# Cross-attention and quantized feed-forward on one core: scores in two float32r parts by pairs of heads, and one ring of seven PSUM banks

## The chip, the cores and the metric

The kernel runs on one core of a Trainium2 chip, in one launch. The metric is the time of an execution on the device in microseconds (us); given is the median of three runs.

## What is computed

There are 16 batches of 512 tokens with 256 values, and for each batch a context of 1601 rows with 192 values. All is float32.

```
x = x + xattn(layernorm(x), ctx)          # 16 heads of 16 values
x = x + ffn(layernorm(x))
xattn: Q = tokens @ Wq; K = ctx @ Wk; V = ctx @ Wv
       softmax(Q K^T * 16**-0.5) V, heads joined, @ Wo + bo
ffn:   fp4_linear(silu(fp4_linear(x, w_gate)) * fp4_linear(x, w_up), w_down)   # 704 wide
       fp4_linear rounds both operands to 4-bit values in blocks of 16, each block with its own scale
```

## The kernel before

**Bodies, groups, steps.** After a start (first context, projections and maxima) there is one body for each batch (first, middle, last), and then a tail for the last batch's feed-forward. A body has four groups of four heads (`PHASES`, `PER_GROUP`), and a group has 13 steps (`KEY_TILES`), each for 128 keys (65 in the last): 52 steps. A step computes, for four heads, the scores of 128 keys against all 512 queries (L901), ACT's exponential of each (L1028), and one step later the sums of the values weighted with them (L912), the four heads in four column strips of the array, with a column of ones beside the values for the softmax's denominator.

**Shift.** So that the exponential can't overflow, each query's largest score is taken off. It is found one group ahead: for each head, four tiles of 128 queries and four pieces of 400 or 401 keys, PE computes the scores the other way round (a "piece", L926, 64 a group) into a ring of three banks, and DVE reduces each to its maximum (L1264). `max_parts` (L1165 to L1173) is five DVE operations that take the maximum over the pieces and cut its negative into three bf16 parts; the round `maxima` transposes them on PE (L845), ACT copies them (L998), and one DMA puts them as three more rows under the stacked queries of the next group (L725), to be multiplied with rows of ones under the keys. The first score of a group waits for this DMA.

**Parts.** Keys and queries are cut into three bf16 parts each (`SPLITS`): ACT copies the projection out of PSUM twice (L984, L987), and POOL takes off and rounds in three operations (L1343 to L1347). SP's DMAs stack the parts of a head in 96 rows, parts of the query repeated 3, 2 and 1 times against the matching parts of the key (`STACK`, L641, L715): six issues a head. A buffer holds four heads and one spare for each parity of the group.

**Rounds.** All other matmuls and transposes are rounds (projections of queries, keys and values, transposes of the context, and for the batch before the output projection and the feed-forward's parts). They use two `work` banks in turn and are drained by ACT or DVE. Float32r operands, with high and low parts, are in the key and value projections (L832, L840) and in the gate and up projection (L865).

**Order.** Every engine walks the same list and does its own part of each item, in order; nothing is reordered at run time. The tables `POST_AT`, `OWN_AT`, `PRE_AT`, `TAIL_AT` and others say at which half step an event is put; an event's rounds are put with it. `sequence` (L277) spreads four scores, the pieces, the rounds and the weighted sums over the step by their cost (`SCORE_PLACE`, `PIECE_WEIGHT`). Scores have a ring of two banks of their own, pieces three, rounds two, and the weighted sums one.

Of the kernel before, what the change touches and what calls it, by code (L numbers as in the profile page):

```python
# [24 lines left out]
F32 = mybir.dt.float32  # L25
# [17 lines left out]
STACK = [3, 2, 1]  # L43
SROWS = sum(STACK) * HEAD_DIM
SHIFT = 3
SPLITS = 3
TINY = 1e-12
ONES_PAIR = struct.unpack("<f", struct.pack("<I", 0x3F803F80))[0]
# [16 lines left out]
]  # L65
TAIL_AT = [
# [15 lines left out]
PIECE_FROM, PIECE_TO = 0.0, 22  # L82


PIECE_WEIGHT = [
# [4 lines left out]
]  # L90
SCORE_PLACE = [0.1225, 0.3125, 0.5225, 0.7625]
PIECE_SHIFT = 0.8
# [11 lines left out]
def events(kind, key_tiles, h_pieces):  # L104
# [24 lines left out]
    for g in range(PHASES):  # L129
        loads = [("stack", (g + 1) % PHASES, j) for j in range(1, PER_GROUP)] + [("stack", (g + 2) % PHASES, 0)] * (g % 2)  # L130
        if kind == "last":
            loads = loads[:3] * (g < PHASES - 1) + loads[3:] * (g < PHASES - 2)
# [7 lines left out]
        if g == PHASES - 1:  # L140
            loads[2:2] = [("load_resid", n) for n in ((0, 1, QT, QT + 1) if kind == "last" else (0, 1))]
# [51 lines left out]
def build(nc, x, ctx_768, Wq, Wk, Wv, Wo, bo, w_gate, w_up, w_down, out):  # L193
# [44 lines left out]
    def splits(of, n, k):  # L238

        return count(of, SPLITS * 2 * (CHUNKS + 1), SPLITS * n + k)  # L240

# [10 lines left out]
    def banks_free(n, ring, per_group):  # L252

        if n >= ring:
            return n - ring + 1
# [1151 lines left out]
```

## Time and profile before

| | |
|---|---|
| median of three runs | 3501.74 us (3499.99 to 3502.39) |
| span of the profiled execution, first to last instruction | 3497.6 us |
| that execution's own time | not given apart from its span |
| mean granted TensorE clock | 0.992 |
| busy: PE, PE weight loads, DVE, ACT, POOL | 97%, 45%, 83%, 66%, 29% |
| chain that ended last: PE, DVE, ACT | 77%, 17%, 2% |
| HBM read and written | 46.22 MB, 8.39 MB |

PE is TensorE's matmuls, PEld its weight loads, DVE VectorE, ACT ScalarE, POOL GpSimd and SP the queue that issues DMAs. Matmuls are pipelined: each has a duration longer than the time until the next one starts, so the distance of two starts tells what one occupies. A row with xN merges N instructions that follow or overlap.

### The profile page before, as it was taken

How to read it: one execution, taken by the hardware profiler on the slowest of the kernel's cores; microseconds unless marked ns; L12 is line 12 of the kernel's file. 1: busy time of each engine (PE TensorE's matmuls, PEld its weight loads, DVE VectorE, ACT ScalarE, POOL GpSimd, SP SyncE). 2: the span in 40 equal slices, each digit the busy share in tenths (PEclk: the TensorE clock that was granted, in tenths of full speed). 3: DMA queues.
4: the chain of work that ended last, by engine and by line, in shares of the span. 5: the costliest groups of instructions: out<-in, count | busy, mean ns of one | idle time of the engine just before them, and what ended most of it. 6: DMA issues, size and time to landing. Idle time of an engine off the chain costs nothing.

```text
span 3497.6 us, 55854 instructions
## 1 busy us (share of the span) xinstructions
PE 3402.9 (97%) x19606; PEld 1557.8 (45%) x19606; DVE 2900.8 (83%) x6561; ACT 2299.7 (66%) x4512; POOL 1001.4 (29%) x1114
## 2 busy tenths in 40 slices
PE   6999999999999999999999999999999999999997
PEld 3334444444444444444444444444444444444434
DVE  6878888888888988888888888988888888888865
ACT  2667666666666667666667666666666666666662
POOL 1323322333222323222333322333222333222213
PEclk8999999999999999999999999999999999999999
DMA  4333233232233332233232232332232231332310
GB/s 85 55 51 50 36 55 54 30 63 41 44 51 46 52 45 47 39 58 49 36 63 34 49 54 36 62 45 42 44 58 44 41 62 30 52 54 32 42 24 8
DMA packets 154262, 163.01 MB, mean 47 GB/s; under 512 B 58071, under 2 KB 127080, under 8 KB 153984
## 3 DMA queue, kind: packets, MB, share of 16 engines
q1 hardware_dynamic: 153984, 159.45, 28.9%
q8 instruction: 157, 2.57, 0.3%
q14 instruction: 121, 0.99, 0.1%
HBM read 46.22 MB, written 8.39 MB: 16 GB/s over the span
## 4 chain that ended last, share of the span: by engine, by line
PE 77%; DVE 17%; ACT 2%; POOL 1%; DMA 1%; issue 1%; SPq 1%; ACTq 0%; DVEq 0%
PE out_ps L912 19%; PE score_ps L901 18%; PE piece_ps L926 17%; DVE piece_max L1264 10%; PE work L865 6%; PE work L876 4%; PE work L832 3%; PE work L840 3%; ACT probs L1028 1%; PE work L821 1%; PE work L856 1%; PE work L873 1%; DVE ctx_T L1134 1%; PE work L850 1%; DVE stats L1107 1%
## 5 line engine op out<-in xcount | busy, mean ns | idle before, releaser
L1028 ACT ACTIVATE probs<-score_ps 128x512 f32<-128x512 f32 (+1 forms) x3328 | 1883.9, 600 | 900.0 <-PE score_ps L901 892.0
L1264 DVE TENSOR_REDUCE piece_max<-piece_ps 128x1 f32<-128x400 f32 (+1 forms) x4096 | 2113.3, 566 | 381.2 <-PE piece_ps L926 367.9
L926 PE MATMUL piece_ps<-k_stack,q_stack 96*128 96x400 bf16 (+1 forms) x4096 | 1291.3, 338 | 27.1 <-DVE piece_max L1264 12.6
L901 PE MATMUL score_ps<-q_stack,k_stack 99*128 99x512 bf16 (+1 forms) x3328 | 1251.7, 384 | 19.3 <-DMA q_stack<-neg_rows 5.2
L912 PE MATMUL out_ps<-probs,v_ones 128*17 128x512 f32 x6656 | 876.6, 599 | 0.4
L926 PEld LDWEIGHTS piece_ps<-k_stack,q_stack 96*128 96x128 bf16 x4096 | 385.1, 98 | 768.9 <-DVE piece_max L1264 514.7
L901 PEld LDWEIGHTS score_ps<-q_stack,k_stack 99*128 99x128 bf16 (+1 forms) x3328 | 324.2, 99 | 646.7 <-ACT probs L1028 494.5
L1316 POOL TENSOR_TENSOR h<-h,h_grid 128x704 f32<-128x704 f32 (+1 forms) x68 | 101.4, 1492 | 881.2 <-DVE h_grid L1092 881.2
L865 PE MATMUL work<-wgu_T,xq_T 128*128 128x512 f32 (+1 forms) x1080 | 333.8, 426 | 0.5
L912 PEld LDWEIGHTS out_ps<-probs,v_ones 128*17 128x17 f32 x6656 | 110.3, 95 | 270.3 <-issue 214.6
L865 PEld LDWEIGHTS work<-wgu_T,xq_T 128*128 128x128 f32 x1080 | 198.1, 191 | 44.0 <-issue 3.8
L1343 POOL TENSOR_TENSOR rest<-rest,k_parts 128x512 f32<-128x512 f32 (+1 forms) x127 | 128.5, 1012 | 266.6 <-ACT rest L987 266.6
L832 PE MATMUL work<-ctx_T,wk_sb 128*128 128x512 f32 (+1 forms) x640 | 199.2, 423 | 5.3 <-DVE ctx_T L1134 2.9
L876 PE MATMUL work<-wd_T,h_T 128*128 128x256 f32 x744 | 190.5, 378 | 0.8 <-ACT h_T L1018 0.8
L840 PE MATMUL work<-wv_sb,ctx_T 128*128 128x256 f32 (+1 forms) x1040 | 187.8, 314 | 1.9 <-DVE wv_sb L1124 1.9
L840 PEld LDWEIGHTS work<-wv_sb,ctx_T 128*128 128x128 f32 (+1 forms) x1040 | 150.4, 188 | 21.2 <-issue 2.8
L876 PEld LDWEIGHTS work<-wd_T,h_T 128*128 128x128 f32 x744 | 138.9, 190 | 25.9 <-ACT h_T L1016 1.0
L1355 POOL TENSOR_TENSOR rstd<-mean_var,eps 128x1 f32<-128x1 f32 x64 | 15.1, 235 | 458.7 <-DVE mean_var L1198 458.7
L1316 POOL TENSOR_TENSOR xq<-xq,h_grid 128x256 f32<-128x256 f32 x60 | 40.2, 670 | 360.8 <-DVE h_grid L1092 360.8
L1008 ACT ACTIVATE tanh_g<-work 128x256 f32<-128x256 f32 (+1 forms) x192 | 70.4, 367 | 102.9 <-PE work L865 100.8
L832 PEld LDWEIGHTS work<-ctx_T,wk_sb 128*128 128x128 f32 x640 | 115.0, 194 | 28.9 <-issue 3.2
L1347 POOL TENSOR_TENSOR k_parts<-rest,k_parts 128x512 bf16<-128x512 f32 (+1 forms) x127 | 114.4, 901 | 9.9
(170 smaller groups left out, 2711.4 us busy)
## 6 DMA issues: line engine op xcount, KB each, us to landing
k_stack<-k_parts SPq DMA_DIRECT2D x256, 150.1 KB, 3.6
k_stack<-k_parts SPq DMA_DIRECT2D x256, 100.1 KB, 3.9
ctx_in<-in_ctx SPq DMA_DIRECT2D x47, 384.0 KB, 3.7
k_stack<-k_parts SPq DMA_DIRECT2D x256, 50.0 KB, 3.7
q_stack<-q_parts SPq DMA_DIRECT2D x256, 48.0 KB, 2.8
x_in<-in_x SPq DMA_DIRECT2D x16, 512.0 KB, 5.0
q_stack<-q_parts SPq DMA_DIRECT2D x256, 32.0 KB, 2.1
resid<-in_x SPq DMA_DIRECT2D x62, 128.0 KB, 3.3
```

The lines of the kernel that those rows point to most:

```text
L832: last = pe.matmul(work[:, 0:w], wk_sb[:, by, e * P:(e + 1) * P], ctx_T[:, of, a:a + w], start=(n == 0), stop=(n == len(PRODUCTS) - 1))
L840: last = pe.matmul(work[0:r, u * D:(u + 1) * D], ctx_T[:, of, a:a + r], wv_sb[:, by, :], start=(n == 0), stop=(n == len(PRODUCTS) - 1))
L865: last = pe.matmul(work[:, 0:w], quarter(kind, t).xq_T[:, of, k, :], wgu_T[:, k, by, a:a + w], start=(k == n == 0), stop=(k == 1 and n == ...
L876: last = pe.matmul(work[:, 0:D], quarter(kind, event[1]).h_T[:, c, :], wd_T[:, c, :], start=(c == 0), stop=(c == FT - 1))
L901: pe.matmul(score_ps[0:r, n % SCORE_RING, :], k_stack[:, par, slot(g, j), m * P:m * P + r], q_stack[:, par, slot(g, j), :], start=True, st ...
L912: last = pe.matmul(out_ps[32 * j:32 * j + V1, :], v_ones[0:r, batch % 2, m, PER_GROUP * g + j, :], probs[0:r, step % 2, j, :], start=(m == ...
L926: pe.matmul(piece_ps[:, n % PIECE_RING, 0:hi - lo], q_stack[0:SROWS, par, slot(g, j), t * P:(t + 1) * P], k_stack[0:SROWS, par, slot(g, j) ...
L1028: act.activation(probs[0:r, step % 2, j, :], score_ps[0:r, (PER_GROUP * m + j) % SCORE_RING, :], ACT.Exp, scale=SCORE_SCALE).then_inc(prob ...
L1264: dve.tensor_reduce(piece_max[:, row, c:c + 1], piece_ps[:, n % PIECE_RING, 0:piece_at[c + 1] - piece_at[c]], AX_X, ALU.max).then_inc(piec ...
L1316: pool.tensor_tensor(src, src, grid, ALU.add).then_inc(done, 1)
L1343: pool.tensor_tensor(left, left, parts[:, 0, a:a + w], ALU.subtract).then_inc(split_step, 1)
L1347: pool.tensor_tensor(parts[:, 2, a:a + w], left, parts[:, 1, a:a + w], ALU.subtract).then_inc(split_step, 1)
```

## The change

Keys and queries are cut into two float32r parts. ACT still copies the projection twice, and POOL has one operation. A head has 48 rows (the query's high part twice and low part once, against the key's high, low and high) and two rows for the shift, which has two float32r parts, too. Of each pair of heads the even one lies in rows 0 to 49, the odd one in rows 64 to 113, of five buffers that the pairs use in turn; scores and pieces of a pair stand next to each other in the list. `max_parts` has three operations, and the shift goes out in four DMAs. All of PSUM but the bank of the weighted sums is one ring of seven, taken in the order of the list: each score, piece or round claims the bank that the seventh one before it used, and waits for its drain. Pieces are 402 wide, the last overlapping. A step's order is now fixed, and the tables are new.

```diff
-STACK = [3, 2, 1]
-SROWS = sum(STACK) * HEAD_DIM
-SHIFT = 3
-SPLITS = 3
+SROWS = 3 * HEAD_DIM
+SHIFT = 2
+HALF = P // 2
+PAIRS = PER_GROUP // 2
+PAIR_SLOTS = 5
 POST_AT = [
+    [4, 5, 5, 9, 13, 14, 19, 20, 20, 21, 23, 23, 23, 26, 33, 34, 38],
+    [22, 23, 23, 23, 32, 37, 38, 43, 45, 45, 48, 48, 51, 51, 56, 62, 65],
+    [52, 55, 55, 58, 59, 59, 65, 66, 66, 66, 68, 69, 70, 73, 78, 80, 85],
+    [74, 74, 74, 74, 74, 78, 82, 86, 86, 87, 87, 93, 95, 95, 100, 101, 102],
 ]
-OWN_AT = [8, 13, 14, 16, 18]
-PRE_AT = [26, 28, 31, 33, 37, 37, 41, 42, 46, 47, 48, 49, 59, 62, 66, 69, 71, 73, 80, 85, 94, 94]
-STACK0_AT = [15, 65]
-LN1 = 5
-HEADS_OUT_AT = 1
+OWN_AT = [6, 13, 14, 17, 18]
+PRE_AT = [26, 28, 29, 30, 37, 37, 47, 48, 51, 51, 54, 55, 59, 62, 66, 69, 69, 70, 78, 83, 87, 91]
+STACK0_AT = [17, 71]
+LN1 = 6
+HEADS_OUT_AT = 3
 MAX_AT = [22, 23]
+PIECES_AT = [
+    [3, 3, 4, 3, 2, 3, 3, 3, 3, 3, 2, 0, 0],
+    [3, 3, 3, 2, 3, 3, 4, 3, 3, 3, 2, 0, 0],
+    [3, 3, 3, 2, 3, 3, 3, 3, 3, 3, 3, 0, 0],
+    [3, 3, 4, 4, 4, 1, 3, 3, 2, 3, 2, 0, 0],
 ]
+STEP_ORDER = "S01 P W01 P S23 P V"
+RINGS, RING_FOR = (7,), (0, 0, 0)
+MERGE = (False, False)
...
+                for what in STEP_ORDER.split():
+                    if what == "P":
+                        take = -(-left // (2 * slots)) * 2
+                        left, slots = left - take, slots - 1
+                        for _ in range(take):
+                            put(0, "piece", (g + 1) % PHASES, n)
...
-        k_stack = sb("k_stack", [SROWS + SHIFT, 2, PER_GROUP + 1, KW], BF16)
-        q_stack = sb("q_stack", [SROWS + SHIFT, 2, PER_GROUP + 1, NQ], BF16)
+        k_stack = sb("k_stack", [P, PAIR_SLOTS, KW], F32R)
+        q_stack = sb("q_stack", [P, PAIR_SLOTS, NQ], F32R)
...
-        piece_ps = ps("piece_ps", [P, PIECE_RING, 512], F32)
-        score_ps = ps("score_ps", [P, SCORE_RING, 512], F32)
+        ring = ps("ring", [P, BANKS, 512], F32)
         out_ps = ps("out_ps", [P, 512], F32)
-        work_ps = ps("work", [P, 2, 512], F32)
...
+            def stack_keys(of, g, u):
+                at = pair_slot(of, g, u)
+                for half in range(2):
+                    rows, to = pair_rows(g, u, half)
+                    sp.dma_start(k_stack[to:to + 2 * HEAD_DIM, at, 0:NK].bitcast(F32), k_parts[rows, :, 0:NK]).then_inc(stacked[at], 16)
+                    sp.dma_start(k_stack[to + 2 * HEAD_DIM:to + SROWS, at, 0:NK].bitcast(F32), k_parts[rows, 0, 0:NK]).then_inc(stacked[at], 16)
...
                 elif name == "maxima":
+                    for j in range(PER_GROUP):
+                        to = HALF * (j % 2) + SROWS
+                        row = q_stack[to:to + SHIFT, pair_slot(of, g, j // 2), :].bitcast(F32).rearrange("n (t c) -> n t c", c=P)
+                        sp.dma_start(row, neg_rows[SHIFT * QT * j:SHIFT * QT * (j + 1), :]).then_inc(shift_loaded[g % 2], 16)
...
+            def claim(kind, batch, item):
+                user = bank_user(kind, batch, item)
+                if user:
+                    pe.wait_ge(*released(*user))
...
+                item = ("scores", step, j)
+                claim(kind, batch, item)
+                rows = slice(lo, lo + SROWS + SHIFT)
+                pe.matmul(ring[0:r, bank(kind, batch, item), :], k_stack[rows, at, m * P:m * P + r], q_stack[rows, at, :],
+                          start=True, stop=True).then_inc(scores_ready, 1)
...
+                claim(kind, batch, item)
+                rows, (a, b) = slice(lo, lo + SROWS), piece_at(c)
+                pe.matmul(ring[:, bank(kind, batch, item), 0:PW], q_stack[rows, at, t * P:(t + 1) * P], k_stack[rows, at, a:b],
+                          start=True, stop=True).then_inc(pieces_ready, 1)
...
-                        for par in range(2):
-                            for j in range(PER_GROUP):
-                                act.wait_ge(stacked[par][j], count(batch, 2 * KSTACKED, KSTACKED * (1 if half else 2)))
+                        first = pair(of, 2 * half, 0)
+                        for k in range(first - 2 * PAIRS, first):
+                            act.wait_ge(stacked[k % PAIR_SLOTS], stacked_until(k))
...
-                    pool.tensor_tensor(left, left, parts[:, 0, a:a + w], ALU.subtract).then_inc(split_step, 1)
-                    pool.tensor_tensor(parts[:, 1, a:a + w], left, zero[:].broadcast_to([P, w]), ALU.add).then_inc(split_step, 1)
-                    pool.tensor_tensor(parts[:, 2, a:a + w], left, parts[:, 1, a:a + w], ALU.subtract).then_inc(split_step, 1)
+                    pool.tensor_tensor(low.bitcast(F32R), low, parts[:, 0, a:a + w], ALU.subtract).then_inc(split_step, 1)
```

In `STEP_ORDER`, S01 and S23 are the scores of a pair, P a third of the step's pieces (`PIECES_AT` counts them in pairs), W01 the events of the step with their rounds, and V the weighted sums of the step before. `POST_AT` has a row for each quarter of 128 tokens of the batch before and a place for each of heads_T, out_proj, ln2_stats, ln2_apply, xq_max, xq_scale, xq_T, three gate_up, h_max, h_small, h_scale, h_grid, two h_T and down; `OWN_AT` places one query and four key projections of the batch's second half, and `PRE_AT` two x_T, eight ctx_T, two v_proj, one query and four key projections and five v_proj of the next batch.

## Rows read from the trace of the kernel before

**Rows 1.** The page, parts 1 and 2: busy time of engines; PE's tenths in 40 slices.

```profile
PE 3402.9 (97%) x19606; PEld 1557.8 (45%) x19606; DVE 2900.8 (83%) x6561; ACT 2299.7 (66%) x4512; POOL 1001.4 (29%) x1114
...
PE   6999999999999999999999999999999999999997
```

**Rows 2.** Stages: us, then busy PE, PEld, DVE, ACT, POOL, clock, DMA share, GB/s.

```profile
0.00:75.00 75.00, 47.12 (x195) 27.87 (x196) 48.19 (x112) 16.78 (x34) 13.61 (x25) 0.85 0.39 78
...
1479.00:1690.00 211.00, 209.46 (x1227) 96.37 (x1223) 179.04 (x406) 143.15 (x282) 61.52 (x69) 1.00 0.30 47
```

**Rows 3.** Groups by line, 1479 to 1690: count | busy us, mean ns | idle before.

```profile
L926 PE MATMUL piece_ps<-k_stack,q_stack 96*128 96x400 bf16 (+1 forms) x256 | 80.5, 337 | 0.6 <-DVE piece_max L1264 0.2
L901 PE MATMUL score_ps<-q_stack,k_stack 99*128 99x512 bf16 (+1 forms) x208 | 78.1, 384 | 0.6
```

**Rows 4.** The chain that ended last, in order of time: start us, us, what.

```profile
361.74 1.93 DVE piece_max L1264 x4
...
3102.83 1.93 DVE piece_max L1264 x4
...
1490.71 0.59 SPq L715
1491.34 0.78 SPq L715
1492.16 3.13 DMA q_stack<-neg_rows
```

**Rows 5.** Timeline of PE, 1501 to 1504: start us, us, what.

```profile
1501.59 0.38 PE L901 MATMUL score_ps<-q_stack,k_stack 99*128 99x512 bf16 x1
1501.89 1.05 PE L912 MATMUL out_ps<-probs,v_ones 128*17 128x512 f32 x8
...
1502.34 0.61 PE L912 MATMUL out_ps<-probs,v_ones 128*17 128x512 f32 x4
1502.88 0.68 PE L926 MATMUL piece_ps<-k_stack,q_stack 96*128 96x401 bf16 x3
1503.40 0.38 PE L901 MATMUL score_ps<-q_stack,k_stack 99*128 99x512 bf16 x1
```

**Rows 6.** Timeline of PE, 223 to 225; three of the four transposes again, alone.

```profile
223.84 0.34 PE L926 MATMUL piece_ps<-k_stack,q_stack 96*128 96x401 bf16 x1
224.11 0.46 PE L883 MATMUL work<-ident,h 64*128 64x64 f32 x4
224.50 0.60 PE L901 MATMUL score_ps<-q_stack,k_stack 99*128 99x512 bf16 x2
...
224.11 0.40 PE L883 MATMUL work<-ident,h 64*128 64x64 f32 x3
```

**Rows 7.** Timeline of PE: three float32r matmuls, and the first two of them.

```profile
1513.77 1.01 PE L865 MATMUL work<-wgu_T,xq_T 128*128 128x512 f32 x3
...
1513.77 0.78 PE L865 MATMUL work<-wgu_T,xq_T 128*128 128x512 f32 x2
```

**Rows 8.** Timeline of PEld: three float32r weight loads, and the first two of them.

```profile
1484.38 0.46 PEld L832 LDWEIGHTS work<-ctx_T,wk_sb 128*128 128x128 f32 x3
...
1484.38 0.34 PEld L832 LDWEIGHTS work<-ctx_T,wk_sb 128*128 128x128 f32 x2
```

**Rows 9.** Timeline of DVE in the start, 44 to 71.

```profile
43.91 25.11 DVE L1264 TENSOR_REDUCE piece_max<-piece_ps 128x1 f32<-128x400 f32 x52
...
69.81 0.17 DVE L1171 TENSOR_TENSOR neg_parts<-piece_ps,zero 128x16 bf16<-128x16 f32 x1
70.02 0.17 DVE L1173 TENSOR_TENSOR neg_parts<-piece_ps,neg_parts 128x16 bf16<-128x16 f32 x1
```

**Rows 10.** The chain in the start.

```profile
29.59 1.05 POOL k_parts L1345
```

**Rows 11.** Timeline of ACT in the last group.

```profile
3407.65 2.17 ACT L1028 ACTIVATE probs<-score_ps 128x512 f32<-128x512 f32 x4 [0.43 <-PE score_ps L901]
3410.53 2.17 ACT L1028 ACTIVATE probs<-score_ps 128x512 f32<-128x512 f32 x4 [0.71 <-PE score_ps L901]
```

More of the change, by code:

```diff
@@ L249, in build @@
     R_START, R_FIRST, R_BODY = (len(ROUND[k]) for k in ("start", "first", "middle"))
-    PIECE_RING, SCORE_RING = 3, 2
-    def banks_free(n, ring, per_group):
-        if n >= ring:
-            return n - ring + 1
-        return max(b + 1 for b in range(per_group) if b % ring == n) - per_group
+    BANKS = sum(RINGS)
+    RING_OF = {"scores": RING_FOR[0], "piece": RING_FOR[1], "round": RING_FOR[2]}
     def transposes(event):
@@ L325, in sequence @@
         for g in range(PHASES):
-            steps = []
+            ahead = g < PHASES - 1 or kind != "last"
+            n = 0
             for m in range(KEY_TILES):
-                fill, step = [], g * KEY_TILES + m
-                for part in range(2):
-                    es = EVENTS[kind].get(2 * step + part, [])
-                    for e in es:
-                        fill.append((0, ("event", e)))
-                        if e[0] in ROUNDS:
-                            fill += [(c, ("round", e, i)) for i, c in enumerate(round_parts(e))]
-                    if part == 0 and (step or kind != "first"):
-                        fill.append((4 * NQ, ("weighted", step - 1)))
-                steps.append(fill)
@@ L340, in sequence @@
[L340 to L356 removed]
+                step = g * KEY_TILES + m
@@ new lines, in build @@
+    DRAIN = {k: {e: sum(by_vector(k, o) == by_vector(k, e) for o in ROUND[k] if ROUND[k][o] < n) for e, n in ROUND[k].items()} for k in ROUND}
+    BANK_USERS = {}
+    for k in SEQUENCE:
+        BANK_USERS[k] = [[] for _ in RINGS]
+        for item in SEQUENCE[k]:
+            if item[0] in ("scores", "piece"):
+                BANK_USERS[k][RING_OF[item[0]]].append(item)
+            elif item[0] == "round" and item[2] == 0:
+                BANK_USERS[k][RING_OF["round"]].append(("round", item[1]))
@@ new lines, in build, with before, bank @@
+    FIRST_USE = {k: {item: n for users in BANK_USERS[k] for n, item in enumerate(users)} for k in BANK_USERS}
+    def before(kind, batch, per):
+        at = {"start": [], "first": ["start"], "middle": ["start", "first"] + ["middle"] * (batch - 1),
+              "last": ["start", "first"] + ["middle"] * (B - 2), "tail": ["start", "first"] + ["middle"] * (B - 2) + ["last"]}[kind]
+        return sum(per(k) for k in at)
+    def bank(kind, batch, item):
+        of = RING_OF[item[0]]
+        n = before(kind, batch, lambda k: len(BANK_USERS[k][of])) + FIRST_USE[kind][item]
+        return sum(RINGS[:of]) + n % RINGS[of]
@@ new lines, in body_before, with bank_user @@
+    def body_before(kind, batch):
+        if kind == "tail":
+            return "last", B - 1
+        if kind == "first":
+            return "start", -1
+        return "first" if batch == 1 else "middle", batch - 1
+    def bank_user(kind, batch, item):
+        of = RING_OF[item[0]]
+        n = FIRST_USE[kind][item] - RINGS[of]
+        while n < 0:
+            if kind == "start":
+                return None
+            kind, batch = body_before(kind, batch)
+            n += len(BANK_USERS[kind][of])
+        return kind, batch, BANK_USERS[kind][of][n]
@@ new lines, in partner, with merged, follows @@
+    def partner(item):
+        return item[:-1] + (item[-1] + 1,)
+    PLACE = {k: {item: n for n, item in enumerate(SEQUENCE[k])} for k in SEQUENCE}
+    def merged(kind, batch, item):
+        if not MERGE[("scores", "piece").index(item[0])] or item[-1] % 2:
+            return False
+        at = PLACE[kind]
+        return at.get(partner(item)) == at[item] + 1 and bank(kind, batch, partner(item)) == bank(kind, batch, item) + 1
+    def follows(kind, batch, item):
+        return item[-1] % 2 == 1 and merged(kind, batch, item[:-1] + (item[-1] - 1,))
@@ L794, in fill @@
                 name = event[0]
-                work = work_ps[:, work_bank(kind, batch, event), :]
+                work = ring[:, bank(kind, batch, ("round", event)), :]
                 if part == 0:
```

324 lines of the change are left out of this document (153 added, 171 removed), and 16 rows, old and new, of tables (PIECE_WEIGHT, POST_AT, TAIL_AT).

## The prediction

> **What bounds the kernel now.** I read the page first: PE is busy for 97% of the span, DVE for 83%, ACT for 66%, and PE's tenths are nines from end to end [rows 1]. Busy time of pipelined matmuls can overstate, so next comes the table by stage. In 211 us of the middle (one body: a batch of 52 steps) PE is busy 209.46 us, DVE 179.04, ACT 143.15, all at full clock, the upper of TensorE's two levels, 2.4 GHz [rows 2]. Then the groups of that stretch: 208 scores and 256 pieces, and PE waited 0.6 us before either [rows 3]. So in a body what is taken from PE is a gain until DVE, some 30 us behind, becomes the limit. The start, 75 us, has other limits: PE is busy for 47 of them [rows 2]; so has the tail. How long a body is comes from the chain, where the same link returns 13 bodies later: (3102.83 - 361.74) / 13 = 210.9 us [rows 4]. There are 16, the last one shorter.
>
> What a PE instruction occupies is read from starts, not from durations. Three pieces fill the 0.52 from 1502.88 to the score at 1503.40: 0.17 each [rows 5]. Two scores last 0.60, one 0.38 to 0.39: 0.22 each [rows 5, 6]. Between a score's start and the weighted sums behind it lie 0.30, of which its columns take 0.21; the second four of the sums start 0.45 behind the first and the piece 0.54 behind the second [rows 5]. So 0.09 is lost before and 0.09 after them. That is what a change of the array's partition costs (they use it in four columns).
>
> **Part 1, scores and pieces in pairs.** Before: 208 x 0.22 + 256 x 0.17 = 45.8 + 43.5 = 89.3 us of a body. After: float32r, 50 or 48 rows, one of a pair in the lower and one in the upper 64 rows, into different banks. Nothing in the trace runs side by side in rows; bounds for a pair are the time of one matmul and of two. A float32r matmul of 512 columns is 0.23 (two last 0.78, three 1.01) [rows 7]; in proportion 402 columns are 0.19 with a little fixed time. So a pair of scores is 0.23 to 0.46, of pieces 0.19 to 0.38. A float32r weight load costs 0.11: with only 66 columns to stream, two loads last 0.34 and three 0.46 [rows 8]. Two in a row are 0.22, over a pair of pieces and under a pair of scores. I take the lower ends, because the nearest rows, the weighted sums, do run side by side in columns, eight records of 0.60 within 1.05 [rows 5]: 104 x 0.23 + 128 x 0.19 = 48.2 us. Gain 41 us a body. If the two loads of a pair go one behind the other, 128 x 0.03 = 3.8 of it are gone.
>
> Float32r matmuls follow each other at 0.23 though each has its own load of 0.11, so in the whole array a load runs under the matmul before it [rows 7, 8]. The Trainium skill, TensorE: Matmul & The Clock Gate, section Part 3: Packing small matmuls, says that a load overlaps matmuls in flight only where the row group differs. The trace speaks against it; by it the sum would end some 26 us a body higher (the fourth rival has this worked out from rows).
>
> **Part 2, changes of partition.** A step becomes scores, pieces, rounds, pieces, scores, pieces, weighted sums. Rounds use the whole array, so a step with rounds has two more changes. By the new tables 39 of 52 steps have some: 78 changes more. The trace has one excursion of this sort, transposes of 64 rows of the gate weights: they start 0.27 after a piece that takes 0.17, and the score behind starts 0.39 after, where four at 0.06 would take 0.24 (three last 0.40, four 0.46) [rows 6]: 0.10 and 0.15. 78 x 0.12 = 9.4 us. Behind a change nothing hides the first load, 0.11 where it is float32r: at 52 + 39 entries to the halves and most of 39 entries to rounds, 120 x 0.10 = 12 us. Together 21 us lost. Bounds: 10 if loads still hide, 31 if the second half of a block also starts one load late. PE's sum: 210.9 - 41.1 + 21 = 191 us.
>
> **Part 3, DVE and the one ring.** The 256 maxima of a body stay (402 columns for 400). In the start, where DVE sets the pace, 52 take 25.11 or 0.483 each [rows 9]: that is its full pace, and 256 are 124 us. Two of five steps of the running maximum go, 0.21 apart [rows 9], four times: 179.0 - 1.7 = 177 us. PE's 191 is only 14 above, and the two aren't in step: a step with three pairs and no round has 2.0 us on PE and 2.9 on DVE; one with three gate rounds 6 to 8 on PE and 4 to 5 on DVE. The ring adds a wait: item n claims the bank of item n-7, so a late maximum stops scores and rounds queued behind it on PE, and ACT waits for those. PE can run ahead of DVE by some 1.5 us. Adding both up by step, with these prices, and taking the larger of each two steps gives 10 us over PE alone (none if the slack were endless, 18 with no slack). So 201. ACT, 143 us, follows.
>
> **Part 4, shift, stacking, ends.** The next group's first score waits for the maxima's way over DVE, PE, ACT and SP. In the chain it lands at 1492.16 + 3.13, and the chain goes on with the next group's work [rows 4]: no slack there. Two DVE steps less are -0.42; one transfer on SP becomes four, and an issue takes 0.59 to 0.78 [rows 4]: +1.8. Net 1.4 a group at most, 0 where rounds cover it, below nothing hardly: 3 us a body. Behind these issues on SP queue stackings and loads that have half a group of slack. Stacking falls from 24 issues a group to 16, 48 rows of four bytes for 96 of two: the same bytes, hidden by the other pair's pieces; without that cover it were 8 issues and a landing, some 8 us. ACT's wait for the stacked pairs before it overwrites q_parts comes a step earlier, at the third step, 12 us after issue: no cost. POOL's split goes from three operations to one; POOL is at 61.52 of 211 [rows 2], so nothing, except in the start, where the two are in the chain with 1.05 each [rows 10]: -2 us. In the last group, which has no pieces, ACT's four exponentials take 2.17 in a step of 2.87, since the ring of two scores stands still during the weighted sums [rows 11]; seven banks let them run on: 0.4 x 13 = -5 us.
>
> **Sum.** A body 191 + 10 + 3 = 204, 7 less. 15 x -7 = -105, last body -10 (its share and the 5), start -2: 3497.6 - 117 = 3381 of span. The page gives the profiled execution's span; the median of the runs, 3501.7, is 4.1 above it, and I take that as what lies around: 3385.
>
> **Rivals.** *Changes cheap, DVE the limit.* If loads hide behind a change too (10 for 21) a body is 193 to 198: 3220 to 3300. For: bf16 loads hide everywhere. Against: the 0.15 above, longer than the 0.10 going in. Chance 0.2.
>
> *Changes of partition eat the pairs*, the other side: loads one behind the other (+3.8) and every block's second half late (31 for 21), 14 us more, of which DVE's slack gives some back: 211 to 218 a body, 3490 to 3610. The point that decides is the price of a change: 41 - 13 (ring and shift) = 28 us over 78 changes, 0.36 us each with its exposed loads. My sum has 0.27, this rival 0.40 and more. Chance 0.25.
>
> *The halves don't run side by side*: the change then doesn't do what it says. 104 x 0.46 + 128 x 0.38 = 96.5 for 89.3, plus 21 and 3: 240, 3960. Chance 0.05.
>
> *A half's load waits for that half's matmul*, as the page's rule has it: pairs at 0.23 + 0.11 and 0.19 + 0.11, 73.8 us for 48.2; PE 217, with some ring and shift 230: 3800. Against it stand rows 7 and 8 as said. Chance 0.05.
>
> **Chances.** My forecast, 201 to 208 a body, 3340 to 3450, has 0.45. 0.2% is about what a measurement of this kernel can tell from no change. Faster by more: 0.45 + 0.2 less what falls short, 0.64. Within: 0.05. Slower: 0.31. The range leaves out the last two rivals and the edges: 3230 to 3600.
>
> **What would show it.** Right: starts within a pair a few ns apart, pairs 0.23 and 0.19 to 0.22 apart, a body near 204, DVE's share up from 83% to 86%, PE waiting tens of us before pieces for DVE and a few tens at group starts for neg_rows. Wrong: the second of a pair 0.1 behind (loads in line) or 0.2 (no overlap); more than 0.36 lost per change; a body whose PE sum is under DVE's; or the granted clock at the lower level inside a body.

## The result and the profile after

3562.2 us (median of 4 runs, 3544.4 to 3563.2) against 3502.1 us before: ratio 1.0159, 95% interval 1.0137 to 1.0182. Forecast was 3385, faster. The sign was wrong; the range (3230 to 3600) held the time. The profiled execution took 3561.5 us, its span is 3559.8: 1.7 us lie around the span, where the forecast had taken 4.1.

The page of the kernel after: busy time, PE's tenths and the granted clock's.

```profile
PE 3335.2 (94%) x19606; PEld 1692.0 (48%) x19606; DVE 2874.6 (81%) x6429; ACT 2254.1 (63%) x4512; POOL 696.0 (20%) x796
...
PE   7999999999999999999999999999999999999996
...
PEclk6898999999999999999999999999999999999998
```

Against [rows 1] PE does less and the time is longer: PE's share fell from 97% to 94%, and DVE's, which was to rise, fell to 81%. So neither is full. The stages, with the granted clock as third figure from the end:

```profile
0.00:75.00 75.00, 52.22 (x190) 35.87 (x190) 46.87 (x105) 15.47 (x32) 6.50 (x17) 0.65 0.39 77
1500.00:1715.00 215.00, 204.73 (x1258) 104.80 (x1258) 181.07 (x408) 143.45 (x288) 42.82 (x49) 0.99 0.26 47
...
3480.00:3559.00 79.00, 48.49 (x196) 37.10 (x196) 45.95 (x109) 12.25 (x31) 21.00 (x26) 0.81 0.03 9
```

The start ran at 0.65, for 0.85 before [rows 2]. How long a body is comes again from one link of the chain that returns, here 12 bodies later: (3258.88 - 684.23) / 12 = 214.6 us, for 210.9.

```profile
684.23 4.09 PE ring L940 x18
...
3258.88 4.10 PE ring L940 x18
```

Scores, pieces and weighted sums in the timeline of PE (start us, us, what):

```profile
1503.86 0.45 PE L1004 MATMUL ring<-k_stack,q_stack 48*128 48x402 f32 x2
1504.14 0.40 PE L977 MATMUL ring<-q_stack,k_stack 50*128 50x512 f32 x2
1504.38 0.35 PE L1004 MATMUL ring<-k_stack,q_stack 48*128 48x402 f32 x2
1504.66 1.05 PE L990 MATMUL out_ps<-probs,v_ones 128*17 128x512 f32 x8
1505.64 0.51 PE L977 MATMUL ring<-q_stack,k_stack 50*128 50x512 f32 x2
1505.98 0.34 PE L1004 MATMUL ring<-k_stack,q_stack 48*128 48x402 f32 x2
1506.26 1.91 PE L907 MATMUL ring<-ctx_T,wk_sb 128*128 128x512 f32 x10
```

Two pieces last 0.35 together, where one of before lasted 0.34 alone [rows 6]: the halves run side by side. A pair of scores stands 0.24 ahead of what follows; a pair of pieces that has a change of partition behind it 0.28, of which 0.19 are its columns, so 0.09 for the change, as before [rows 5]. The scores at 1505.64 stand 0.34 ahead of their followers, 0.10 more than in steady state: the way back costs as much again.

**An account by instruction.** For each kind of neighbour (score behind score, piece behind score, ...) I took the distance of the ends of two PE instructions; the lower quartile of each kind at the full clock is its price, and the prices of a body add up to "PE's own sum". What exceeds it is a wait, or, in stretches at the lower level, loss to the clock. Means of 14 bodies (the second to the fifteenth), us:

| | body | PE's own sum | waits | lost to the clock | time at the lower level |
|---|---|---|---|---|---|
| before | 210.9 | 204.6 | 6.3 | 0.0 | 0.0 |
| after | 214.5 | 182.2 | 24.4 | 7.9 | 16.3 |
| difference | +3.6 | -22.4 | +18.1 | +7.9 | |

Forecast: own sum -20 (41 less 21), waits +13 (ring 10, shift 3), clock 0. So the computing became as cheap as forecast, and 2 us more; the waits, 5 more than forecast, and the clock, 7.9 that the forecast didn't have, gave it all back. Fifteen bodies of +3.6 make 54 of the 60 us; the first score starts 4.0 us later (77.3 for 73.3).

Who made PE wait, from the waits over the whole execution (us in total, times, longest us):

```profile
PEld ring L1004 <- DVE piece_max L1336: 177.6, 467, 1.8
PEld ring L977 <- DVE piece_max L1336: 170.3, 234, 1.7
...
PEld ring L977 <- ACT probs L1106: 129.5, 228, 1.7
PEld ring L977 <- DMA q_stack<-neg_rows: 77.7, 49, 4.0
...
PE ring L977 <- DMA q_stack<-neg_rows: 36.2, 32, 4.2
```

Weight loads that would have waited unseen behind matmuls count here too, so these are shares and not the sum. Three releasers stand out: the maxima, the exponentials, the shift. By kind, 12.2 of the 24.4 us of a body lie between pieces, 4.1 between the two pairs of scores of steps without rounds (the ring's seventh item back is a score of the same step, whose exponential isn't done), 2.0 before the first score of a group.

**Where the clock falls.** The boundary from the second to the third group of one body. SP's queue, then PE's timeline, then three windows:

```profile
2529.86 2.68 SPq L796 DMA_DIRECT2D q_stack<-neg_rows  x4
2532.58 0.62 SPq L715 DMA_DIRECT2D q_stack<-q_parts  x1
```

```profile
2531.94 1.05 PE L990 MATMUL out_ps<-probs,v_ones 128*17 128x512 f32 x8
2533.69 0.50 PE L977 MATMUL ring<-q_stack,k_stack 50*128 50x512 f32 x2 [0.69 <-ACT probs L1106]
...
2535.40 0.64 PE L928 MATMUL ring<-ident,heads 128*128 128x128 f32 x2 [1.02 <-DVE ctx_T L1211]
...
2537.36 1.91 PE L990 MATMUL out_ps<-probs,v_ones 65*17 65x512 f32 x8
```

```profile
2523.69:2533.69 10.00, 8.74 (x60) 3.05 (x53) 9.37 (x22) 8.57 (x19) 0.44 (x1) 1.00 0.04 9
2533.69:2536.69 3.00, 1.98 (x10) 1.28 (x12) 1.39 (x3) 1.46 (x3) 2.84 (x3) 0.79 0.59 91
2537.20:2546.60 9.40, 9.40 (x42) 6.56 (x40) 4.30 (x12) 3.27 (x6) 0.68 (x2) 0.55 0.37 55
```

Four issues take 2.68 us, the score waits 0.7 and the transposes behind it 1.0, and then for some 10 us the granted clock is at the lower level, 1.2 GHz: the eight weighted sums take 1.91 for 1.05. PE counts as busy for the whole of that window, so its busy time in the table of stages holds this loss too. The Trainium skill, TensorE: Matmul & The Clock Gate, section A second HAM failure mode: psum-queue depth-cycling, has this mechanism: a kernel that cycles through banks leaves PE idle for short times so often that its clock goes back and forth between the two levels. The trace has the same picture (waits 24.4 us a body, 16.3 us at the lower level); which of the waits brings the clock down the experiments below don't show. It is a rule that I should have set against the forecast.

### The profile page after: what moved, and what is told of

It reads as the page before. It is cut to its first block, busy times and chain, and to the rows that moved or that the text cites. A ratio compares the mean times of both kernels' runs of the same rounds, so it can differ in the third digit from the quotient of the medians.

```text
span 3559.8 us, 55150 instructions
## 1 busy us (share of the span) xinstructions
PE 3335.2 (94%) x19606; PEld 1692.0 (48%) x19606; DVE 2874.6 (81%) x6429; ACT 2254.1 (63%) x4512; POOL 696.0 (20%) x796
## 4 chain that ended last, share of the span: by engine, by line
PE 79%; DVE 11%; ACT 4%; SPq 2%; DMA 2%; issue 1%; POOL 0%; DVEq 0%; POOLq 0%
PE out_ps L990 19%; PE ring L1004 15%; PE ring L977 15%; PE ring L940 7%; DVE piece_max L1336 6%; PE ring L951 5%; PE ring L915 4%; PE ring L907 4%; ACT probs L1106 3%; PE ring L931 2%; SPq L796 2%; PE ring L948 2%; DMA q_stack<-neg_rows 2%; PE ring L925 1%; PE ring L896 1%
## 5 line engine op out<-in xcount | busy, mean ns | idle before, releaser
L1336 DVE TENSOR_REDUCE piece_max<-ring 128x1 f32<-128x402 f32 x4096 | 2069.7, 567 | 303.2 <-PE ring L1004 291.2
L1106 ACT ACTIVATE probs<-ring 128x512 f32<-128x512 f32 (+1 forms) x3328 | 1794.6, 600 | 696.7 <-PE ring L977 677.8
L1004 PE MATMUL ring<-k_stack,q_stack 48*128 48x402 f32 x4096 | 886.0, 406 | 50.6 <-DVE piece_max L1336 34.0
L977 PE MATMUL ring<-q_stack,k_stack 50*128 50x512 f32 (+1 forms) x3328 | 844.9, 474 | 46.9 <-DMA q_stack<-neg_rows 36.2
L977 PEld LDWEIGHTS ring<-q_stack,k_stack 50*128 50x128 f32 (+1 forms) x3328 | 350.7, 187 | 881.0 <-issue 277.3
L1004 PEld LDWEIGHTS ring<-k_stack,q_stack 48*128 48x128 f32 x4096 | 468.9, 196 | 321.3 <-DVE piece_max L1336 177.6
L940 PE MATMUL ring<-wgu_T,xq_T 128*128 128x512 f32 (+1 forms) x1080 | 250.4, 383 | 1.8
L940 PEld LDWEIGHTS ring<-wgu_T,xq_T 128*128 128x128 f32 x1080 | 193.9, 188 | 52.5 <-issue 21.4
L915 PE MATMUL ring<-wv_sb,ctx_T 128*128 128x256 f32 (+1 forms) x1040 | 176.7, 321 | 1.9 <-DVE wv_sb L1201 1.9
L951 PE MATMUL ring<-wd_T,h_T 128*128 128x256 f32 x744 | 176.5, 387 | 2.0
```

Source lines behind the costliest of these rows:

```text
L915: last = pe.matmul(work[0:r, u * D:(u + 1) * D], ctx_T[:, of, a:a + r], wv_sb[:, by, :], start=(n == 0), stop=(n == len(PRODUCTS) - 1))
L940: last = pe.matmul(work[:, 0:w], quarter(kind, t).xq_T[:, of, k, :], wgu_T[:, k, by, a:a + w], start=(k == n == 0), stop=(k == 1 and n == ...
L951: last = pe.matmul(work[:, 0:D], quarter(kind, event[1]).h_T[:, c, :], wd_T[:, c, :], start=(c == 0), stop=(c == FT - 1))
L977: pe.matmul(ring[0:r, bank(kind, batch, item), :], k_stack[rows, at, m * P:m * P + r], q_stack[rows, at, :], start=True, stop=True).then_i ...
L1004: pe.matmul(ring[:, bank(kind, batch, item), 0:PW], q_stack[rows, at, t * P:(t + 1) * P], k_stack[rows, at, a:b], start=True, stop=True).t ...
L1106: act.activation(probs[0:r, step % 2, j:j + n, :], ring[0:r, at:at + n, :], ACT.Exp, scale=SCORE_SCALE).then_inc(probs_ready, n)
```

## The experiments

All times are to be set beside 3562 (after) and 3498 to 3504 (before, on the same chip). Figures of a body are means over the same 14 bodies, by the same account. The times in the table are of one run each, and runs of one program spread: after from 3544 to 3563, r6's program from 3483 to 3533 (r17). A difference of some 30 us between two single times says little.

| | time | body | own sum | waits | lost to clock | at lower level |
|---|---|---|---|---|---|---|
| r1_three_rings | 4394.6 | 262.6 | 176.9 | 56.8 | 29.0 | 54.9 |
| r2_half_maxima | 3422.0 | 206.5 | 181.9 | 19.8 | 5.0 | 9.7 |
| r3_shift_one | 3494.2 | 210.0 | 182.0 | 22.3 | 5.7 | 10.5 |
| r4_full_rows | 3719.2 | 225.1 | 216.9 | 8.2 | 0.2 | 0.2 |
| r5_merge | 3690.2 | 222.0 | 180.5 | 30.6 | 11.1 | 20.5 |
| r6_shift_queues | 3504.7 | 210.1 | 182.4 | 24.3 | 3.4 | 6.3 |
| r7_sums_middle | 3747.8 | 225.3 | 184.1 | 28.0 | 13.4 | 26.8 |
| r8_fillers | 3589.4 | 216.5 | 185.6 | 23.4 | 7.5 | 16.6 |
| r9_pieces_placed | 3537.0 | 212.3 | 182.5 | 26.9 | 2.9 | 5.9 |
| r10_sums_after_rounds | 4012.2 | 243.3 | 178.4 | 48.3 | 16.6 | 35.4 |
| r11_both | 4012.3 | 243.4 | 177.1 | 55.9 | 10.5 | 23.4 |
| r12_ring_six | 3942.8 | 238.8 | 181.6 | 44.9 | 12.3 | 24.9 |
| r13_rounds_split | 3598.5 | 216.3 | 179.8 | 32.5 | 4.0 | 8.8 |
| r14_stock | 3648.7 | 220.1 | 176.6 | 35.2 | 8.4 | 15.4 |
| r15_ln1_later | 3534.0 | 212.6 | 182.5 | 24.7 | 5.3 | 11.0 |
| r16_pieces_after_sums | 3588.8 | 216.1 | 185.2 | 25.6 | 5.3 | 11.5 |

The split into own sum and waits has a margin. r2, r3, r6 and r12 have the list of after, and their own sums are 181.6 to 182.4; r1 has it too and comes out at 176.9. So in a kernel that waits a lot, some 5 us may stand in the wrong column.

**r4: the pairs taken away.**

```diff
-                rows = slice(lo, lo + SROWS + SHIFT)
+                rows = slice(0, P)
...
-                rows, (a, b) = slice(lo, lo + SROWS), piece_at(c)
+                rows, (a, b) = slice(0, P), piece_at(c)
```

> Edit: scores and pieces take all 128 rows (the unused rows are zero), so both heads of a pair are summed, nothing runs side by side, and there are no more changes of partition than before; the exponential's scale is 0 so that it stays finite. Columns cost 208 x 0.23 + 256 x 0.19 = 96.4 us a body against 46.7 in pairs. If a change of partition costs what the trace says (18.6 us a body), PE's sum is 182 + 49.7 - 18.6 = 213, with few waits and the full clock 217 to 222 a body: 3600 to 3680 us. Rival C (the changes cost 0.36 us and more each, exposed loads included, 28 us or more): 3560 or less, at or under the changed kernel.

Every score and piece uses all rows (the unused ones zeroed, the exponentials' scale 0). Longer than expected. PE at 216.9 is the limit as before, waits 8.2. If pairs cost one after the other, the own sum should rise by 48.2 (the forecast's columns once more) or 49.7 (with the fixed times measured); it rose by 34.7. The missing 15.0 us are the changes of partition that went with them: 0.19 for each of the 78. The trace of after has the same price directly, by the distance of ends: the first gate and up matmul of 512 columns ends 0.43 behind a piece and 0.23 behind another of its kind, a pair of pieces 0.37 behind rounds and 0.18 behind scores, so 0.20 each way.

The forecast's 21 us can't be set beside these 15, since 52 exposed loads behind the weighted sums are in them, which r4 keeps: the first score ends 0.43 behind the sums in r4 and in after, 0.32 before, so 5 us a body. For the 78 changes alone the forecast had 21 - 5 = 16, or 0.20 each. In its own terms, loads included, 15 + 5 = 20 us came for 21, 0.26 a change for 0.27 (and 0.40 in the opposing rival). Parts 1 and 2 of the forecast stand. The Trainium skill, TensorEngine Tiling (Array Packing), section Key Properties, says that a change of tiling mode drains TensorE, without a figure; the traces agree that a change costs, 0.19 to 0.20 each here.

**r1: three rings.** `RINGS, RING_FOR = (2, 3, 2), (0, 1, 2)`, as many banks for scores, pieces and rounds each as before the change.

> Edit: the changed kernel with three rings again, two banks for scores, three for pieces, two for rounds, in place of one ring of seven. Theory A (the gain of the pairs is lost in waits of the one ring, in which a late DVE maximum also holds up scores and rounds): own rings free the scores from the maxima, a body goes from 215 to about 205, 3400 to 3470 us. Rival B (DVE and PE are out of step whatever the ring, and three banks hold fewer maxima in flight than seven do): slower than the changed kernel, 3590 to 3680 us. Rival C (the price of the changes of partition decides): within 1% of 3562.

All three theories fail: 4394.6, waits 56.8. Rival B had the direction, slower than after, and was far short. Its largest waits of PE:

```profile
PEld ring L1004 <- DVE piece_max L1336: 676.0, 1108, 3.1
PEld ring L977 <- ACT probs L1106: 619.6, 759, 1.7
```

Pairs take two banks at once. With two for scores the second pair waits for both exponentials, with three for pieces the second pair waits for a maximum. So the change needs the one ring, or at least more than these shares of seven (no other shares were run); that kinds share it is not what makes the waits.

**r2: half a maximum.** `piece_max` reads 201 of 402 columns (half of each piece takes no part in the maximum).

> Edit: each DVE maximum reads only 201 of a piece's 402 columns, so that half of the keys is left out of the maxima; PE's work is the same. It takes about 0.21 us from each of 4096 maxima. Theory A (waits for DVE, and the lower clock that comes with them, ate the gain): waits of PE fall from 24 us a body to under 10 and most of the 17 us at the lower clock go, a body of 190 to 197, 3190 to 3300 us. Rival C (changes of partition ate it): within 1% of 3562.

-140 us, between the theories: about half of the least that theory A expected, but far more than 1%. Its waits over the whole execution:

```profile
PEld ring L977 <- ACT probs L1106: 180.6, 354, 0.9
PEld ring L977 <- DVE piece_max L1336: 138.2, 164, 0.9
PEld ring L977 <- DMA q_stack<-neg_rows: 84.9, 49, 4.0
PEld ring L1004 <- DVE piece_max L1336: 42.3, 137, 1.2
```

DVE is some 50 us a body lighter, and waits fall by only 4.6 a body: those of pieces for maxima go from 177.6 to 42.3, those of scores for the exponentials rise from 129.5 to 180.6. So DVE's sum alone is not what sets the body: with 128.5 us of DVE in 210 it still took 206.5 us, and the ring waits for its next slow reader.

**r3 and r6: the shift.** r3 loads only the first of the four transfers from the second batch on (the shift of the other three heads stays that of the first batch); r6 keeps all four and has two issued by ACT, behind the copy that makes neg_rows:

```diff
-                    for j in range(PER_GROUP):
+                    for j in range(PAIRS):
...
+                    act.wait_ge(*drained(kind, batch, event))
+                    for j in range(PAIRS, PER_GROUP):
...
+                        act.dma_start(row, neg_rows[SHIFT * QT * j:SHIFT * QT * (j + 1), :]).then_inc(shift_loaded[g % 2], 16)
```

> Edit: from the second batch on only the first of the four transfers of the shift is issued, so that three heads of a group keep an old shift. If the longer way of the shift decides (Rival D: three issues, 1.8 us a group, and PE at the lower clock after them): 64 x 1.8 = 115 us and some clock, 3400 to 3450 us. Theory A: the wait is 2 us a body by the trace, with the clock perhaps 5: 3480 to 3540 us.

> The four transfers of the shift are issued by two engines, two by SP and two by ACT, everything else as in the changed kernel. Theory A (the shift's four issues in a row on one queue make the first score of a group late, and the wait, after those for the rounds at the boundary, brings the lower clock in the third group): the third group's median falls from 60.8 to 56-58 us, lower-clock time per body from 16 to 11-13 us, total 3495 to 3535. Rival B (the landing counts and not the issue, and ACT's issues delay its exponentials by about as much): 3550 to 3580.

Both times are as theory A had them: -68 and -58 us. The time at the lower level in r6 fell further than expected (6.3 us, for 11 to 13). The same boundary in r6:

```profile
2482.69 1.47 SPq L796 DMA_DIRECT2D q_stack<-neg_rows  x2
```

```profile
2482.70 1.28 ACTq L1079 DMA_DIRECT2D q_stack<-neg_rows  x2
```

```profile
2485.16 1.05 PE L990 MATMUL out_ps<-probs,v_ones 128*17 128x512 f32 x8
2486.14 0.50 PE L977 MATMUL ring<-q_stack,k_stack 50*128 50x512 f32 x2
```

The transfers are out 1.2 us sooner, and the score no longer waits: 0.98 behind the weighted sums for 1.75. The third group's median went from 60.8 to 56.1. Waits as a sum hardly changed (24.3 for 24.4), but their places did. The 2.0 us a body before the first scores are gone; 1.0 came up before the weighted sums, which wait for the exponentials of ACT, now with two issues of its own in between. Over the whole execution, first after, then r6:

```profile
PE out_ps L990 <- ACT probs L1106: 1.4, 6, 0.3
```

```profile
PE out_ps L990 <- ACT probs L1113: 16.0, 24, 1.2
PE ring L977 <- DMA q_stack<-neg_rows: 5.5, 2, 4.0
```

What the body won, 4.4 us, is the clock's 4.5 (7.9 to 3.4). That the wait for the shift alone brings the clock down is not so: r4 waits for the same transfers nearly as long as after (36.2 us there), and has 0.2 us a body at the lower level.

```profile
PE ring L979 <- DMA q_stack<-neg_rows: 31.0, 34, 4.2
```

So the wait of 2.0 us cost 4.4 in a body that has many others, while in r4, where PE has few, it brought no lower clock. Why it does in the one and not in the other isn't shown.

**r17: r6 again, timed.**

> r6_shift_queues again, timed in five rounds against the kernel before. Theory A (the shift's queue explains some 1.6% of the changed kernel's time, and no more is won): 3490 to 3515, ratio to before 0.997 to 1.004, to the changed kernel 0.981 to 0.987. Rival B (its one look had a lucky clock): 3520 to 3560.

3502.5 us (12 runs, 3483.5 to 3533.3), before 3501.1 (17 runs): ratio 1.0001, interval 0.9978 to 1.0023. The whole loss against before is gone, and nothing is won. Its twelve runs are one program and differ in the granted clock: mean 0.971 in the shortest (span 3481.7), 0.956 in the longest (3531.5). Twice the share missing from 1 times the span is the time at the lower level: 202 and 311 us. A line through all twelve has a slope of 0.42 us of time for 1 us at the lower level (correlation 0.985).

**r8: PE kept busy at the boundary.** Four float32r matmuls into the claimed bank ahead of the wait for the shift.

> Four extra float32r matmuls of 512 columns (0.23 us each) into the bank that the first score of a group has claimed, ahead of its wait for the shift; they leave no trace in the output. Theory A (TensorE's idle time at the boundary brings the lower clock): time at the lower clock falls from 16.3 us a body to 8 or less, and the body is 1 to 4 us shorter, 3495 to 3550, although 3.7 us of work were added, half of it where PE waited anyway. Rival B (the idle time before the boundary is not what lowers the clock): lower-clock time stays 14 to 18 us a body and the body becomes 1.5 to 3.7 us longer, 3580 to 3620.

Rival B, by the figures: time at the lower level 16.6 for 16.3. The third group got shorter (58.8 for 60.8), but the first longer (54.6 for 51.1), with lower-level stretches there instead. That the idle time right at the wait brings the clock down is not confirmed; work put into the gap did not prevent it.

**r12: a bank less.** `RINGS = (6,)`.

> The changed kernel with a ring of six banks instead of seven, nothing else. Theory A (PE's waits come from the shallow ring: how far PE can run ahead of VectorE's maxima and ACT's exponentials is what decides): PE's own sum stays at 182, waits rise from 24.4 to 33-42 us a body, with more time at the lower clock; total 3700 to 3900. Rival B (VectorE's sum and the places of its bursts decide, a bank more or less is little): waits 25 to 28, total 3570 to 3640.

3942.8: theory A in its direction, and above its range. Over the whole execution:

```profile
PEld ring L977 <- DVE piece_max L1336: 563.1, 631, 2.2
...
PEld ring L977 <- ACT probs L1106: 195.0, 413, 1.7
```

Own sum the same, waits +20.5, clock +4.4: one bank less is worth 24 us a body. So how far PE can run ahead decides, and that is a count of banks: a block of one pair of scores and two of pieces takes six of the seven. How much of the 24.4 us of waits a deeper ring would take away was not run; with the bank of the weighted sums all eight are in use. r4 has the ring of seven too, and waits 8.2 us: by these runs the ring makes PE wait much only once PE's own sum comes near that of its readers.

**r5: one maximum for a pair.** `MERGE = (False, True)`.

> One maximum of VectorE reads both banks of a pair of pieces (128 instructions of 804 columns for 256 of 402). Theory A (a ring of seven that waits for VectorE, and the waits lower the clock): fewer fixed costs, VectorE some 8 us a body less (181 to about 173), of the 24.4 us of waits 3 to 6 go and some of the 8 us lost at the lower clock: 3440 to 3510. Rival B (grain matters more than sum: the first bank of a pair comes free only when the second is read, half a maximum later): waits as before or more, 3550 to 3600.

Rival B, and worse: 3690.2. Fewer instructions on DVE, but both banks of a pair come free together and late: waits 30.6 for 24.4. With a shallow ring the grain matters more than DVE's sum.

**r7, r10, r16: other orders of the step.** `"S01 P V P S23 P W01"`, `"S01 P W01 V P S23 P"`, `"S01 P W01 S23 P V P"` for `"S01 P W01 P S23 P V"` (S scores, P pieces, W rounds, V weighted sums; r10 and r16 on top of r6).

> Order of a step: two scores, pieces, weighted sums, pieces, two scores, pieces, rounds. The number of changes of partition is the same, only the places differ. Theory A (scores of one step wait for the exponentials of the step's first scores, because seven items lie between; the weighted sums between them add time): the waits of scores for ACT (0.57 us in steps without rounds) shrink, but the sums come one half step sooner after the last exponentials and wait for them instead. Total within 1.5% of the changed kernel, 3510 to 3600. Rival B (weighted sums now wait for the last exponentials of every step, about 0.6 us in 52 steps, and nothing is won): a body is 10 us or more longer, 3680 to 3850.

> The shift issued by two engines, and the order of a step: two scores, pieces, rounds, weighted sums, pieces, two scores, pieces. The rounds and the weighted sums then stand side by side, so a step with rounds has three changes of partition for four, and the pieces of the end run into the next step's scores without one. Theory A (each change costs 0.15 to 0.2 us): TensorE's own sum falls from 182.4 to 175-178 us a body; the waits stay (24) or grow by 2 to 6, since VectorE and ACT get their work in longer bursts: 3430 to 3500. Rival B (burstier supply costs more than the change saves, as r7_sums_middle, which came out 15 us a body longer with its scores waiting for ACT): 3550 to 3700.

> Base is r6_shift_queues (3505). Order of a step: two scores, pieces, rounds, two scores, pieces, weighted sums, pieces. The place for pieces between rounds and scores moves behind the weighted sums; as many changes of partition as before. Theory A (with seven banks the longest stretch without pieces decides: now it is the 1.7 us from the weighted sums' start over the next two scores, which this order cuts to 1.3): waits fall by 2 to 5 us a body, 3430 to 3480. Rival B (the order of the changed kernel is even already, every other order starves VectorE or the exponentials elsewhere, as in the three orders tried): 3550 to 3800.

All three lost: +186 us on after, +508 and +84 on r6. r7 and r16 came out as their rival B had them, r10 beyond its rival. In r10, 39 changes of partition are gone: the weighted sums follow the rounds, and the first of them ends 0.53 behind a round as it does behind a piece, so each step with rounds saves one way back of 0.20. That makes 8 us; the account shows 4.0, within its margin. DVE's timeline shows what else came:

```profile
2798.04 1.06 DVE L1343 TENSOR_REDUCE piece_max<-ring 128x1 f32<-128x402 f32 x2 [2.57 <-PE ring L1004]
...
2800.21 3.00 DVE L1343 TENSOR_REDUCE piece_max<-ring 128x1 f32<-128x402 f32 x6 [0.29 <-PE ring L1004]
```

2.57 us without work, then six maxima in a row, while PE waits for banks: waits 48.3. In r16 waits between pieces fell (12.2 to 7.7), those between scores rose (4.2 to 8.9).

**r9, r11, r13, r14, r15: other places for pieces and for the normalisation** (all on top of r6). r9: `PIECES_AT` follows the difference of PE's and DVE's work by step; r11: r9 with r10's order; r13: `"S01 P W0 P W1 P S23 P V"`; r14: two pairs ahead of the rounds, one behind, none ahead of the weighted sums; r15: `LN1 = 19` for 6.

> The shift issued by two engines (as in r6_shift_queues), and the pairs of pieces placed so that VectorE's work of a step follows TensorE's: fewer pieces in steps where VectorE scales and quantises, more in steps with long rounds. The same instructions, other places. Theory A (the 12 us a body of waits between pieces come from VectorE's bursts in single steps, not from its sum): those waits fall from 12.2 us to 4-7 us a body, a body from 210 to 202-205 us, total 3385 to 3450. Rival B (VectorE's sum with ACT's share sets the body, the places hardly matter): 3480 to 3510.

> Both edits together: places of r9_pieces_placed, order of r10_sums_after_rounds. If their effects are apart (places: waits of VectorE; order: changes of partition) the gains add up: 3330 to 3420. If the order's bursts undo what the places win: 3480 to 3650.

> Base is r6_shift_queues (3505). The rounds of a step are parted in two with pieces between them where both halves have some: finer grain for VectorE, two more changes of partition in some 20 of 52 steps. Theory A (VectorE is starved during long rounds and then gets its maxima in a burst): waits fall from 24.3 to 17-20 us a body, TensorE's own sum rises by 4 to 8; total 3460 to 3530. Rival B (the waits sit in steps without rounds): waits 23 to 25, total 3560 to 3620.

> Base is r6_shift_queues (3505). In steps with rounds two pairs of pieces stand ahead of the rounds, one behind them, none ahead of the weighted sums (before: one at each place). The number of changes of partition stays. Theory A (a stock of four banks keeps VectorE busy during the rounds): waits fall by 3 to 8 us a body, total 3390 to 3470. Rival B (four pieces at once run into the ring, and the step's end leaves VectorE idle through the weighted sums): waits rise, as in r10_sums_after_rounds, total 3550 to 3800.

> Base is r6_shift_queues (3505). The next batch's first normalisation (2 us of VectorE in a burst) moves from the fourth and fifth step of the first group, where PE then waits 1.7 us between pieces, to the tenth and eleventh, which have the longest rounds. Theory A: that wait goes, group 1's median falls by 1 to 1.8 us, total 3475 to 3495. Rival B (it only turns up at another step): 3500 to 3520.

None helped. r9 (+32 us on r6's 3504.7; waits 26.9) misses theory A by far: what a step holds in sum doesn't matter when the ring bridges only part of a step. r11 ends where r10 does, beyond both its theories. r13 and r14 both leave the place ahead of the weighted sums empty, and the waits between pieces go from 12.2 to 20.6 and 23.6: DVE starves through the sums. In r15, 1.3 of the 1.7 us at the sixth step did go (4.3 to 3.0 us), and other steps of the group became longer: the second by 1.3 us, the tenth by 1.1, the twelfth by 1.6. Its time (3534.0) and r9's (3537.0) lie just above the spread of r6's program, so for these two only the figures of the body tell. None of the eight other orders and placements beats the changed kernel's even spread, each set beside the kernel that it was built on.

**Waits and clock over all kernels.** Before and r4 wait 6 and 8 us a body and have 0.0 and 0.2 at the lower level; the six that wait 20 to 25 on the kernel after's order (r2, r3, r6, r8, r15, after) 6 to 17; r12, r10, r1 (45, 48, 57) 25, 35, 55. The order isn't strict (r9: 27 and 6; r13: 33 and 9; r11: 56 and 23). That waits bring the lower level is borne out as a trend and by where the stretch in r6's third group went; which wait does and which doesn't stays open.

## Why the prediction was wrong

- **Part 1**, pairs, 41 us: right. Two in 0.35, a pair of scores 0.24, and [rows 7, 8] were the right basis: no loads one behind the other. The rule of the Trainium skill that I had set against them (TensorE: Matmul & The Clock Gate, Part 3: Packing small matmuls) does not hold for these float32r loads: by it PE's own sum would have been 217 us by my working, and it is 182. The rivals "The halves don't run side by side" and "A half's load waits for that half's matmul" are out: r4 shows what the first would look like.
- **Part 2**, changes of partition, 21 us: right: some 20 us for 21, as worked out under r4. The opposing rival "Changes of partition eat the pairs" has the measured body and time in its ranges (211 to 218, 3490 to 3610) by luck: the point that was to decide, 0.36 us a change with its loads, is not reached (0.26).
- **Part 3**, the ring, +10: one of the two steps that failed, here in size. I added the work of DVE and PE by step and let the slack be 1.5 us, two steps long. r12 shows that the slack is a count of banks, r2 that the exponentials hold banks too, which my working left out, r5 and r10 that order within a step decides. Measured with the shift: +18.1 for +13; the first scores' wait for the shift is 2.0 of it, so the ring has some 16 for 10. "Changes cheap, DVE the limit" is out too: the changes cost 20 us, not 10, a body is 214.5, not 193 to 198, and DVE at half its maxima gives 8 us.
- **Part 4**, shift +3: mechanism right, size off. The four issues took 2.68 us, as the 0.59 to 0.78 of [rows 4] said; the wait at the first scores is 2.0 us a body in sum, for 3 forecast. With what the clock added, r6 won 4.4 us a body by splitting the issues. The last group's gain was right: from its first score to its last 35.7 us for 41.4 (-5.7, forecast -5). ACT is then the limit:

```profile
3467.57 7.08 ACT L1106 ACTIVATE probs<-ring 128x512 f32<-128x512 f32 x14
```

  The start got 4.0 us longer, not 2 shorter, at a clock of 0.65 for 0.85; the stretch behind the last score is 8 us longer (71 to 80), at 0.81 for 0.88.
- **The clock**, 0 in the sum: the other step that failed, and the larger one. The term was put at nothing without a reason, and named only among what would make the forecast wrong. I took PE's full clock in the body [rows 2] as given, though the change takes from PE the busy time that went with it. It costs 7.9 us of every body by the account. After has 395 us at the lower level, before 55; at r17's slope the 340 us are some 143 us, against a loss of 60. At before's clock the change would have been near 3420: faster. That is an estimate with the slope of r6's program; no run was at that clock. The page on the clock gate (the Trainium skill, TensorE: Matmul & The Clock Gate, section Terms) has half a us lost per us at the lower level; r17 has 0.42; that PE waits anyway in part of the time at that level would explain it, and is not shown.

In sum: 201 + 3 = 204 was forecast, 182.2 + 24.4 + 7.9 = 214.5 came. Of the 10.5 us between them the clock has 7.9 and the waits 5.1, and the own sum takes 2.4 back.

## What to carry to other kernels

When a change takes work from an engine that is full, price what it will wait for next in buffers, not in sums: count the banks that a block takes against those that there are, with every reader that holds one, and ask what the order within a step does. Then ask what clock the less busy engine will be granted: here each us at the lower level cost 0.42. Look also at how small transfers on a critical chain are issued: here four on one queue, split over two, moved the time by 1.6%.

## What the runs showed of the hardware

- Float32r matmuls of 50 and 48 rows in the lower and the upper 64 rows run side by side with their weight loads: two in 0.34 to 0.35 us, where one bfloat16 matmul of 96 rows took 0.34.
- A change between matmuls in row halves and matmuls in the whole array costs 0.20 us each way, a float32r load that nothing hides included (by the distance of ends in after; 0.19 from r4).
- The granted clock falls to the lower level inside a body in which PE is busy for over 90% of the time: 16.3 us of each 214.5. In r4, with waits of 8.2 us a body for 24.4, it is 0.2 us.
- The same program on the same chip in twelve runs spread by 1.4% (3483.5 to 3533.3) with the granted clock; the kernel before, whose clock hardly moves (0.989 to 0.993), by 0.2%.
- One bank of PSUM less cost 24.3 us of a body of 214.5, 11%.
